# Encoder: attention output turned by VectorE block transposes instead of TensorE, LayerNorm applied by ScalarE and GpSimd

## What is computed

```
q, k, v = x @ Wq + bq, x @ Wk + bk, x @ Wv + bv          # 16 heads of 16, D = 256
q, k = elu(q) + 1, elu(k) + 1
# causal linear attention in chunks of 128 tokens
A     = tril(q_chunk @ k_chunk.T);  intra = A @ v_chunk
inter = q_chunk @ KV                                      # KV: sum of k.T @ v over earlier chunks
a     = (intra + inter) / (denominator + 1e-6)            # the denominator by the same two sums
x = layer_norm(x + a @ Wo + bo, g1, be1)
y = gelu(x @ W1 + b1) @ W2 + b2                           # DFF = 1024
x = layer_norm(x + y, g2, be2)
```

## Time and profile before

| | |
|---|---|
| runs | 1614.22, 1612.58, 1613.78 us |
| median | 1613.78 us |
| span of the profiled execution | 1609.4 us; its own device time is not among the runs listed |
| TensorE busy | 1523.1 us, 95% |
| VectorE, ScalarE, GpSimd busy | 1287.7 (80%), 951.3 (59%), 802.8 (50%) |
| encoder's steps | from about 77 to 1200 us |
| DMA | 82.52 MB, mean 51 GB/s |

### The profile page before, as it was taken

How to read it: one execution, slowest core, us unless ns; L and a number is a source line. 1 busy time by engine, 2 the same in 40 slices (tenths; PEclk the granted TensorE clock), 3 DMA queues, 4 the chain that set the end, 5 groups by cost and what they waited for, 6 DMA issues and landing times.

```text
span 1609.4 us, 38530 instructions
## 1 busy us (share of the span) xinstructions
PE 1523.1 (95%) x15894; PEld 1225.0 (76%) x15894; DVE 1287.7 (80%) x2566; ACT 951.3 (59%) x1516; POOL 802.8 (50%) x580
## 2 busy tenths in 40 slices
PE   3799999999999999999999999999998999999998
PEld 3688888888888888888888888888886566666434
DVE  3777888888888888888878878888776788988556
ACT  3465556665556665565655556655534777777445
POOL 3354445545455454554555535654455366664424
PEclk8899999999999999999999999999999999999999
DMA  6110011201121001210012100112024444443001
GB/s 137 37 62 15 21 24 41 66 9 21 25 67 46 5 19 24 67 47 11 12 24 67 47 19 11 18 41 50 1 49 121 138 136 139 143 139 95 1 0 53
DMA packets 98351, 82.52 MB, mean 51 GB/s; under 512 B 23040, under 2 KB 86400, under 8 KB 98176
## 3 DMA queue, kind: packets, MB, share of 16 engines
q1 hardware_dynamic: 98176, 80.06, 18.5%
HBM read 50.78 MB, written 14.68 MB: 41 GB/s over the span
## 4 chain that ended last, share of the span: by engine, by line
PE 83%; DVE 11%; issue 2%; ACT 1%; SPq 1%; POOL 1%; DMA 0%; ACTq 0%; DVEq 0%
PE e_pr L170 10%; PE e_pr L172 8%; PE e_pr L171 8%; PE e_tr L428 6%; PE e_sc L401 6%; PE x_psO L1366 4%; PE e_tr L170 4%; PE e_tr L172 3%; PE e_tr L171 3%; PE e_sc L170 3%; PE e_sc L172 3%; PE e_sc L171 3%; PE e_tr L438 3%; PE x_psT L1351 2%; PE f_bank L1912 2%
## 5 line engine op out<-in xcount | busy, mean ns | idle before, releaser
L715 POOL TENSOR_TENSOR e_h_lo<-e_h_f,e_h_hi 128x512 fp32r<-128x512 f32 x192 | 265.7, 1388 | 279.1 <-ACT e_h_hi L557 275.2
L805 DVE TENSOR_TENSOR e_am<-e_sc,c_amask 128x1024 f32<-128x1024 f32 x192 | 225.7, 1216 | 18.3 <-PE e_sc L401 18.3
L556 ACT ACTIVATE e_h_f<-e_pr,e_h_bias 128x512 f32<-128x512 f32 x192 | 132.1, 688 | 174.3 <-PE e_pr L172 170.6
L1676 DVE TENSOR_REDUCE x_mx<-x_psS 128x4 f32<-128x1024 f32 x128 | 150.9, 1219 | 25.8 <-PE x_psS L1329 24.9
L170 PE MATMUL e_tr<-e_W_hi,e_h_hi 128*128 128x256 f32 x576 | 163.2, 283 | 8.1 <-DVE X L762 8.1
L170 PE MATMUL e_pr<-e_yT_hi,e_W_hi 128*128 128x512 f32 x384 | 168.6, 439 | 0.0
L171 PE MATMUL e_tr<-e_W_lo,e_h_hi 128*128 128x256 f32 x576 | 160.8, 279 | 0.0
L172 PE MATMUL e_tr<-e_W_hi,e_h_lo 128*128 128x256 f32 x576 | 160.7, 279 | 0.0
L172 PE MATMUL e_pr<-e_yT_hi,e_W_lo 128*128 128x512 f32 x384 | 152.3, 397 | 0.0
L171 PE MATMUL e_pr<-e_yT_lo,e_W_hi 128*128 128x512 f32 x384 | 151.8, 395 | 0.0
L1502 ACT ACTIVATE x_ex<-x_psT 128x1024 f32<-128x1024 f32 x128 | 130.9, 1022 | 26.5 <-PE x_psT L1351 21.6
(11 more groups left out here) (284 smaller groups left out, 4320.5 us busy)
## 6 DMA issues: line engine op xcount, KB each, us to landing
e_raw_m<-in_L_attn_W_dram SPq DMA_DIRECT2D x12, 1024.0 KB, 5.3
x_qs<-query_rows SPq DMA_DIRECT2D x48, 256.0 KB
e_x_raw<-e_a_tok SPq DMA_DIRECT2D x368, 32.0 KB, 1.9
x_ks<-key_rows SPq DMA_DIRECT2D x48, 128.0 KB, 2.8
query_rows<-x_q_hi SPq DMA_DIRECT2D x16, 256.0 KB, 2.1
query_rows<-x_q_lo SPq DMA_DIRECT2D x16, 256.0 KB, 2.3
x_ctok<-in_ctx_dram SPq DMA_DIRECT2D x8, 256.0 KB, 3.3
x_xo<-in_x_dram SPq DMA_DIRECT2D x8, 256.0 KB, 3.8
```

The lines of the kernel that those rows point to most:

```text
L556: act.activation(h_f[:, m % HR, :], ps_pr[m % 2][:, :], ACT.Gelu, bias=h_bias[:, m:m + 1])
L715: pool.tensor_tensor(h_lo[:, m, :], h_f[:, m % HR, :], h_hi[:, m, :].bitcast(F32), ALU.subtract).then_inc(h_lo_done, 1)
L805: dve.tensor_tensor(am[:, s % 2, c, :, :, :], ps_sc[:, :, c * 2 * P:(c + 1) * 2 * P].rearrange("p r (h n) -> p r h n", n=P), amask[:, :].u ...
L1676: dve.tensor_reduce(mx[:, N % 2, :, 0:HG].rearrange("p i (a h) -> p h a i", a=2)[:, pair], ps_s[pair][:, :, :].rearrange("p a (i j) -> p a ...
```

## The change

**TensorE.** to_tokens and the eight transposes of a_tok are gone. The inter part runs as 16 matmuls of 32 columns in place of 8 of 64, so that a bank holds the heads in 32x32 blocks. qk(1) of the next tile is made with qk(0), both between the second and third block of Wo. The transposes of yT come in the order c = 1, 0, and the second residual they need is waited for in two parts.

**VectorE.** Four block transposes (128x512) turn each bank of e_tr to ob; denominators, reciprocals and the divide run on pairs of blocks; two block transposes (to_features) turn the result into qkT's free half; attn_lo on pairs. centre and scale of both LayerNorms go (except for the last tile). x_transpose gets its own buffer and moves from before phi's end to behind residual(2, 2).

**ScalarE.** normed(1) after exp(1) and normed(2) after gelu(3) apply (x - mean) * rs to X in four instructions each. The copies of oT go. attn_hi(0) stands behind x_hi(1) and ahead of gelu(5), attn_hi(1) behind gelu(7). W1's hi part is made in a layer's first step; W2's, in the same step, after gelu(2) and gelu(3).

**GpSimd.** The shift of a LayerNorm, the product with g (gained, L751), and be2's row (shifted, L757). be1 and b2 are summed once a layer, so be1 + b2 is one row. bo's row goes from the end of the step to ahead of that row and of all h_lo.

**SP.** In every step the sixteen moves come first. W2 of a layer is loaded in that layer's first step behind them, not in the last step of the layer before.

What moves on three engines, each place shown before and after. GpSimd in a layer's third step (q = 2), before: X<-X,e_b is b2's row, X<-X,e_bo is bo's.

The diff, cut to what the steps above speak of:

```diff
--- before.py
+++ after.py
...
-    oT = sb_att("oT", [2, 4, P])
+    ob = sb_att("ob", [2, H, HP])
...
+    aT, a_nrm = qkT[:, KC:2 * KC, :], ktok[:, :, :, :].rearrange("p b c n -> p b (c n)")
...
-    x_blocks = a_tok[:, :, :].rearrange("p s d -> p (s d)").rearrange("p (c j n) -> p c j n", c=KC, j=NR)
+    x_blocks = sb_att("x_blocks", [KC, NR, TT // NR])
...
@@ sync
-                if l > 0 and q == 1:
-                    sp.wait_ge(ln_done[2], SB * NT * l)
-                    load_rows(l, ["g2", "be2"], rows_m, ln2_rows_loaded)
                 if following:
                     move_x(u + 2)
+                if l > 0 and q == 1:
+                    sp.wait_ge(ln_done[2], NT * l)
+                    load_rows(l, ["g2", "be2"], rows_m, ln2_rows_loaded)
...
+                if l > 0 and q == 0:
+                    sp.wait_ge(w1_lo, l + 1)
+                    load_w2(l)
...
                 if more and q == NT - 1:
-                    sp.wait_ge(ln_done[1], SB * (NT * l + NT))
+                    sp.wait_ge(xb2_done, NT * l + NT)
                     load_rows(l + 1, ["g1", "be1"], rows_a, ln1_rows_loaded)
-                    sp.wait_ge(xb2_done, NT * l + NT)
-                    load_rows(l + 1, ["b2"], rows_m, b2_loaded)
-                    sp.wait_ge(w1_lo, l + 2)
-                    load_w2(l + 1)
+                    load_rows(l + 1, ["b2"], rows_m, ln1_rows_loaded)
@@ tensor
-                    pe.wait_ge(ln_done[1], SB * u + SB)
-                    if prev:
-                        pe.wait_ge(z_done[2], SB * d + 3)
-                    for c in range(KC):
+                    pe.wait_ge(ln_done[1], u + 1)
+                    for c in (1, 0):
+                        if prev:
+                            pe.wait_ge(z_done[2], SB * d + 3 - c)
...
-                        for c in range(KC):
-                            for r in range(NR):
-                                rows, cols = slice(r * RH, (r + 1) * RH), slice((r % 2) * 2 * HP, (r % 2 + 1) * 2 * HP)
-                                pe.matmul(out_block(s, 2 * c + r // 2)[cols, :], kv[rows, s // 2, c, :, :].rearrange("p h d -> p (h d)"),
-                                          qkT[rows, c, blk(s)], start=(c == 0), stop=False, skip_group_check=True)
+                        for g in range(4):
+                            for a in range(NR):
+                                rows = slice(a * RH, (a + 1) * RH)
+                                pe.matmul(out_block(s, g, rows), kv[rows, s // 2, g // 2, g % 2, :], qkT[rows, g // 2, blk(s)],
+                                          start=(g == 0), stop=False, skip_group_check=True)
...
-                def to_tokens(s):
-
-                    pe.wait_ge(oT_done, SB * t + s + 1)
-                    if s > 0:
-                        pe.wait_ge(a_done, SB * t + s)
-                    for g in range(4):
-                        mm = pe.transpose(ps_tr[1][:, blk(g)], oT[:, s % 2, g, :], ident[:, :])
-                    mm.then_inc(tok_full, 1)
...
-                    pe.wait_ge(a_done, SB * t + SB)
-                    for c in range(KC):
-                        for s in range(SB):
-                            mm = pe.transpose(ps_tr[c][:, blk(s)], a_tok[:, s, blk(c)], ident[:, :])
-                        mm.then_inc(aT_tr, 1)
-                if mlp:
                     mlp_up(7)
...
@@ scalar
+                def normed(i, n, tile):
+                    act.wait_ge(rs_done[i], LNS[i] * n + 2)
+                    for s in range(SB):
+                        x = X[:, tile * SB + s, :]
+                        act.activation(x, x, ACT.Identity, bias=shift[i][:, s:s + 1], scale=rs[i][:, s:s + 1]).then_inc(xn_done[i], 1)
...
@@ gpsimd
                 if mlp:
-                    add_row(q, rows_m["b2"], yT_tr, 2 * u + 2, b2_loaded, 16 * (l + 1), xb2_done)
+                    if following:
+                        add_row((q + 2) % NT, rows_a["bo"], xT_tr, t + 3, bo_loaded, 16 * (l2 + 1), xbo_done)
+                    if q == 0:
+                        pool.wait_ge(ln1_rows_loaded, 48 * (l + 1))
+                        pool.tensor_tensor(rows_a["be1"][:, :], rows_a["be1"][:, :], rows_m["b2"][:, :], ALU.add).then_inc(rows_summed, 1)
+                    add_row(q, rows_a["be1"], yT_tr, 2 * u + 2, rows_summed, l + 1, xb2_done)
                     for m in range(FC):
                         if m == 2 and u > 0:
-                            rsqrt(2, ve_done[2], u)
+                            rsqrt(2, u - 1)
...
-                if following:
-
-                    ln = l + 1 if q >= NT - 2 else l
-                    add_row((q + 2) % NT, rows_a["bo"], xT_tr, t + 3, bo_loaded, 16 * (ln + 1), xbo_done)
-                if more and q == NT - 1:
-                    w_m("W1", w1_hi, l + 2, w1_lo)
@@ vector
+                def to_tokens(s):
+                    dve.wait_ge(out_full, SB * t + s + 1)
+                    if s >= 2:
+                        dve.wait_ge(norm_step, NORM * (2 * t) + 3)
+                    dve.transpose(ob[:, s % 2, :, :].rearrange("p g n -> p (g n)"), ps_tr[s % 2][:, :]).then_inc(ob_done, 1)
...
+                def to_features(pair):
+                    n = 2 * t + pair
+                    cols = slice(2 * P * pair, 2 * P * (pair + 1))
+                    dve.wait_ge(norm_step, NORM * n + 3)
+                    dve.transpose(aT[:, :, cols].rearrange("p c (b n) -> p b c n", b=2),
+                                  a_nrm[:, :, :].rearrange("p b (c n) -> p b c n", c=KC)).then_inc(norm_step, 1)
```

More of the change, by code:

```diff
@@ L511, in w_o, with w_m @@
                 act.activation(hi["Wo"][:, :, :], raw_a[:, 3], ACT.Copy).then_inc(o_hi, 1)
-            def w_m(w, done):
+            def w_m(w, done, part):
                 flat = hi[w][:, :, :].rearrange("p c n -> p (c n)")
-                for j in range(4):
+                for j in (2 * part, 2 * part + 1):
                     a = act.activation(flat[:, j * TT:(j + 1) * TT], raw_m[:, j * TT:(j + 1) * TT], ACT.Copy)
@@ L550, in step @@
                         exp(j)
+                        if mlp and j == 1:
+                            normed(1, u, q)
+                elif mlp:
+                    normed(1, u, q)
                 def gelu(m):
@@ L587, in step @@
                                    ACT.Copy).then_inc(ktok_done, 1)
+                if more and q == NT - 2:
+                    act.wait_ge(raw_qkv_loaded, 48 * (l + 2))
+                    act.wait_ge(v_full, 2 * t + 2)
+                    w_qkv(l + 1)
+                if l > 0 and q == 0:
+                    act.wait_ge(raw_1_loaded, 16 * (l + 1))
+                    act.wait_ge(h_full, FC * u)
+                    w_m("W1", w1_hi, 0)
+                    w_m("W1", w1_hi, 1)
+                if q == NT - 1 and attn:
+                    act.wait_ge(raw_o_loaded, 16 * (l + 2))
+                    act.wait_ge(wo_full, SB * t)
+                    w_o(l + 1)
                 if u == final:
@@ L663, in w_o, with w_m @@
                 lo_part("Wo", raw_a[:, 3].rearrange("p c n -> p (c n)"), 1, o_lo)
-            def w_m(w, ready, value, done):
-                pool.wait_ge(ready, value)
-                lo_part(w, raw_m, 4, done)
+            def w_m(w, ready, layer, done, part):
+                flat_hi = hi[w][:, :, :].rearrange("p c n -> p (c n)").bitcast(F32)
+                flat_lo = lo[w][:, :, :].rearrange("p c n -> p (c n)")
+                pool.wait_ge(ready, 2 * layer + part + 1)
+                for j in (2 * part, 2 * part + 1):
+                    cols = slice(j * TT, (j + 1) * TT)
+                    a = pool.tensor_tensor(flat_lo[:, cols], raw_m[:, cols], flat_hi[:, cols], ALU.subtract)
+                if part == 1:
+                    a.then_inc(done, 1)
             w_qkv(1)
@@ L891, in step @@
                                       ALU.add).then_inc(qk_bias_set, 1)
-                if prev:
-                    residual(2, 1, d, last, m_full, xb2_done)
                 if u == final:
@@ L898, in step @@
                     residual(2, 2, d, last, m_full, xb2_done)
-                    for s in range(SB - 1):
-                        spread(2, s, d, last)
+                if following:
+                    x_transpose(t + 1, (q + 2) % NT)
                 if attn:
@@ L917, in step @@
                     moments(2, d)
-                for s in range(SB):
-                    if attn and s + 1 < SB:
-                        mask(s + 1)
-                    if prev and s == 0:
-                        centre(2, d, last, rows_m["g2"], ln2_rows_loaded, rows)
-                    if prev and s == 2 and u < final:
-                        scale(2, d, last, rows_m["be2"], range(0, 2))
-                    if attn:
-                        divide(s)
+                if attn:
+                    mask(1)
+                    to_tokens(0)
+                    mask(2)
+                    to_tokens(1)
+                    denominators(0)
+                    mask(3)
```

(18 more changed lines are left out.)

297 lines of the change are left out of this document (157 added, 140 removed).

## The result

The changed kernel takes 1673.9 us (median of 4 runs, 1671.7 to 1677.2) against 1613.2 before: ratio 1.038, 95% interval 1.0366 to 1.0395. It is slower, as forecast, but by 61 us and not 25, and outside the range. The profiled execution has a span of 1673.0 us, 63.6 more than before.

A forecast was written before the change was run, and what follows sets the result against it. TensorE was taken as the bound. From the span, 1609.4 - 39.8 - 4.6 - 9.5 (layer change) + 17.5 + 55 + 3 - 1.8 + 5.7 = 1634.9; plus 4.4 gives 1639 us, range 1600 to 1662.

The forecast's parts named there:

- bo binds: Third step of every layer but the last: bo's late load holds GpSimd, up(6) and up(7) start late; +55 us.
- Transposes off TensorE: Every step: TensorE saves 2.55 us of transposes, pays 0.82 for doubled inter matmuls; -39.8 us over 23 steps.
- rival 4: VectorE's ring up to to_features(0) bounds every step; slower still, 1664 to 1673 us; chance 0.12.
- W2: First step of five later layers: W2 loads behind the moves, delaying gelu(4), up(6) and up(7); +17.5 us.
- z waits: yT transposes: their first group no longer waits for the third residual, 0.21 us over 22 steps; -4.6 us.
- Small: New ties of scores(3) to mask(2) and of qk(2) to residual; +3 us (0 to +10).
- start and end: First attention step gains, -1.8 us; last step has more GpSimd passes ahead of the cross stage's rows, +5.7.
- Rival 2: Third steps: bo's load lands early enough that its row on GpSimd is covered; 1584 us, chance 0.17.

The follow-up runs named there:

- run 2: The changed kernel with the loads of bv and bo put ahead of the sixteen moves in SP's queue: 1619.6 us.
- run 3: The changed kernel with the load of W2 put ahead of the sixteen moves in a layer's first step: 1651.8 us.
- Run 8: The changed kernel with bv, bo and W2 loaded ahead of the moves, VectorE's h_bias copy gone, q and k bias instructions behind attn_lo(1): 1585.7 us.
- run 7: The changed kernel with bv, bo and W2 loaded ahead of the moves, and GpSimd's gained and shifted on 8 of 1024 columns only: 1579.4 us.
- run 1: The changed kernel with bo's row added by GpSimd at the end of each step again, as before the change: 1659.1 us.

## Why the prediction was wrong, by its own steps

Right were the sign, the deciding mechanism and its size. **bo binds**: +55 forecast, 54 came back in run 2. up(6) began at S+26.0 for S+26. Inside it two sizes were off: the half clock costs nearly 4 us a step and not 1, while up(7) waits 0.54 and not 3. The two cancel, and that the sum came so near is luck.

**Transposes off TensorE**: the group behind an up now starts 1.59 us after the up's first matmul, before with the transposes 2.03 (486.28 - 484.25): the 0.44 of the sum. The block transposes measure 0.70 us, as estimated, and attn_hi(0) is not late outside the slow steps; rival 4's place was not the bound. Its mechanism, VectorE slowed beside GpSimd, was; I had looked for it at mask(3) to to_features(0), and it sits between phi and residual(2,2).

**W2**: +17.5, measured 22 (run 3). The load lands 6 us after its issue, perhaps because four attention weights follow it in the queue, and normed(2) takes 2.07 for 1.5.

**The step that failed: "z waits, -4.6 (0 at worst)".** I took the wait of the yT transposes as given by their order on TensorE and asked nothing about what the change puts on GpSimd ahead of residual(2,2). There stand now 7.2 us a step more (two gained, one shifted), and in a first step W1's lo parts, 6.3. In the quiet steps the wait did go. In the others VectorE, slowed beside GpSimd, brings residual(2,2) late: without the waits for W2 and bo a first step still takes 3.4 us more than a quiet one (run 3), a third 0.9 (run 2), one last step 1.1, together +23 that the sum has at nothing. Run 8, which takes tiny instructions out of GpSimd's reach, gave back 19 us, and run 7, which makes GpSimd's new work small, 18 in the layers. It is largely the same time, so the two do not add. What is left in run 8, 1.2 us over a quiet step in a first step and 0.8 in a third, was not taken apart.

**"Small: +3 (0 to +10)"** was too small as well, and outside its bounds. The quiet steps take 47.1 us and not 46.5 (the 48.44 it starts from is 48.46 by its rows, which changes nothing). Timeline rows show 0.56 of it around Wo: with qk(0) and qk(1) in its middle, the product's four blocks take 3.42 us of TensorE's time for 2.86, 0.3 of it a wait of qk(2) for residual(1,2). Over 23 steps that is +14.

With these in place the sum is -39.8 - 4.6 - 9.5 + 22 + 54 + 23 + 14 - 1.8 + 5.7 = +63.0, and the two spans differ by 63.6. The agreement is closer than the terms are known: start and end, +3.9 in the sum, measure about +1.

Rival 2 put the kernel at 1584 if bo's load were covered. Run 2 covers it and takes 1619.6, because W2, the slowed VectorE and the small term are still there. That run 8 comes to 1585.7 is chance, since it also has W2 early and the small instructions gone. It does show that part of what the change could bring was there, under waits that it made itself.

## What to carry to other kernels

When an instruction is moved up in an engine's queue, look where its load stands in the DMA queue, and what the transfers ahead of that load wait for: two small loads behind sixteen others cost 54 us here, and moving them cost nothing. When work is given to GpSimd, price it not by GpSimd's idle time but by what VectorE runs beside it: list VectorE's instructions with two SBUF inputs, and its copies and scalar operations from SBUF, on the way to the next thing TensorE waits for. And undoing a part of a change (run 1) can show a cost that the part was there to avoid.
